# Early stages of a four-layer cross-attention kernel: first buffers loaded one stage ahead, setup in order of need, output projection of self attention rewritten two batches deep

## What is computed

```
x = rms_norm(hidden_states, ln_in_w)
mixed = where(vm, x @ v_qkv, x @ l_qkv)          # vm: token and its follower both of type 1
q, k, v = heads(split(mixed)); q, k = apply_rotary(q, k)
ctx = sdpa(q, k, v, causal=True)                  # 16 heads of 16
hidden_states = residual + where(vm, ctx @ v_dense, ctx @ l_dense)
ci = rms_norm(hidden_states, ln_post_cross_w)
cq = heads(ci @ cq_w);  ck, cv = heads(split(encoder_outputs @ ckv_w))
cctx = sdpa(cq, ck, cv, causal=False)             # 16 heads of 8, 1601 keys
```

## Time and profile before

| | |
|---|---|
| median of 3 runs | 3840.3 us (3838.75 to 3840.41) |
| profiled execution's own time | 3844.03 us |
| its span | 3842.4 us |
| TensorE busy | 3447.9 us (90% of the span) |
| VectorE, ScalarE, GpSimd busy | 2025.7, 1842.6, 1576.5 us |
| transfers | 179.33 MB, mean 47 GB/s |

### The profile page before, as it was taken

One profiled execution on the slowest core, in us unless ns is written; L12 is line 12 of the kernel. 1 busy time (PEld: TensorE's weight loads), 2 busy tenths in 40 slices (PEclk: granted clock), 3 DMA queues, 4 the chain that ended last, 5 costly groups with the idle time before them and its releaser, 6 DMA issues. The chain is left out here.

```text
span 3842.4 us, 74386 instructions
## 1 busy us (share of the span) xinstructions
PE 3447.9 (90%) x25040; PEld 2329.4 (61%) x25040; DVE 2025.7 (53%) x3336; ACT 1842.6 (48%) x3376; POOL 1576.5 (41%) x1401
## 2 busy tenths in 40 slices
PE   5678667989899979997999999999999997998998
PEld 4534443444444438885666666666666665887886
DVE  3435325777777745543556555555555553113544
ACT  1123223766666753433555555555555554233332
POOL 1201021111122211110777777777777777003554
PEclk9878877999999989998999999999999998999998
DMA  3477120000000012223000000000000001202200
GB/s 96 117 109 106 62 94 4 17 16 16 18 17 17 8 64 105 92 101 119 10 13 32 31 13 32 13 31 13 32 13 30 15 12 58 94 33 105 86 13 12
DMA packets 77020, 179.33 MB, mean 47 GB/s; under 512 B 16864, under 2 KB 46048, under 8 KB 71136
## 3 DMA queue, kind: packets, MB, share of 16 engines
q1 hardware_dynamic: 72928, 161.83, 14.4%
q0 software_dynamic: 3712, 12.59, 1.2%
HBM read 115.09 MB, written 59.26 MB: 45 GB/s over the span
## 5 line engine op out<-in xcount | busy, mean ns | idle before, releaser
L1640 POOL TENSOR_TENSOR cross_acc<-cross_acc,cross_probs 128x512 f32<-128x512 f32 (+1 forms) x704 | 921.4, 1309 | 158.7 <-ACT cross_probs L1703 116.9
L1703 ACT ACTIVATE cross_probs<-cross_s,cross_bias 128x512 f32<-128x512 f32 (+1 forms) x832 | 530.2, 685 | 487.4 <-PE cross_s L1917 481.5
L1798 DVE TENSOR_REDUCE cross_partmax<-cross_r 128x1 f32<-128x400 f32 (+1 forms) x1024 | 540.9, 570 | 336.4 <-PE cross_r L1887 318.4
L1270 DVE TENSOR_REDUCE cross_partmax<-cross_m 128x2 f32<-128x800 f32 (+1 forms) x512 | 498.0, 992 | 201.6 <-PE cross_m L1379 200.6
L1190 ACT ACTIVATE cross_probs<-cross_s 128x512 f32<-128x512 f32 (+1 forms) x832 | 452.1, 596 | 148.4 <-PE cross_s L1399 147.8
L1930 PE MATMUL cross_av<-cross_probs,cross_v 128*64 128x256 f32 (+1 forms) x3328 | 458.3, 393 | 0.0
L1930 PEld LDWEIGHTS cross_av<-cross_probs,cross_v 128*64 128x64 f32 (+1 forms) x3328 | 199.4, 136 | 172.8 <-ACT cross_probs L1703 74.6
L1410 PE MATMUL cross_av<-cross_probs,cross_v 128*32 128x256 f32 (+1 forms) x3328 | 269.4, 396 | 11.5 <-ACT cross_probs L1190 8.9
L1379 PE MATMUL cross_m<-cross_ks,cross_qd 64*128 64x400 f32 (+1 forms) x1024 | 210.6, 416 | 51.3 <-DVE cross_partmax L1270 46.2
L1911 PE MATMUL cross_s<-cross_q_hi,cross_k_hi 64*128 64x256 f32 (+1 forms) x1664 | 253.5, 299 | 0.0
L1116 POOL TENSOR_TENSOR cross_diag<-c_ident,cross_negmax 128x256 fp32r<-128x256 f32 x128 | 75.9, 615 | 420.7 <-DVE cross_negmax L1278 420.7
(11 more groups left out here) (284 smaller groups left out, 6581.6 us busy)
## 6 DMA issues: line engine op xcount, KB each, us to landing
d_masked_ctx<-tail_ctx_split SPq DMA_DIRECT2D x8, 1602.0 KB, 5.2
d_self_qk<-selfproj_qk_split POOLq DMA_DIRECT2D x32, 256.0 KB
d_cross<-tail_pr SPq DMA_DIRECT2D x8, 1024.0 KB, 5.1
cross_qp<-d_cross SPq DMA_DIRECT2D x64, 128.0 KB
d_cross<-cross_out SPq DMA_DIRECT2D x64, 128.0 KB, 1.8
tail_at<-d_cross SPq DMA_DIRECT2D x8, 1024.0 KB, 5.5
self_qs<-d_self_qk SPq DMA_DIRECT2D x56, 128.0 KB, 8.4
self_ks<-d_self_qk SPq DMA_DIRECT2D x56, 128.0 KB, 9.0
```

The source lines that it names most:

```text
L1270: nc.vector.tensor_reduce(partmax[:, :, jt // 2, jt % 2, i:i + 1], m_pair(M_SET[q], w), AX.X, ALU.max).then_inc(maxed, 1)
L1640: nc.gpsimd.tensor_tensor(acc[0:w, g % 2], left, probs[0:w, slot % NPB], ALU.add).then_inc(added, 1)
L1703: nc.scalar.activation(probs[0:w, (g * KT + t) % NPB], src_, ACT.Exp, scale=XHD ** -0.5, bias=bias[0:w, p, t:t + 1]).then_inc(probs_ready, 1)
L1798: nc.vector.tensor_reduce(partmax[:, m, i:i + 1], r_ps[MAX_BANK[q]][:, 0:KCH[i][1]], AX.X, ALU.max).then_inc(maxed, 1)
```

## The change

It has five parts.

1. `Phase` takes a side: alternate stages allocate from the left or the right end of the on-chip memory, so a stage's first buffers (`SelfprojEarly`, `SelfEarly`, `SelfoutEarly`, `Cross0Early`) can exist while the one before still runs.
2. Setup: the loads for the rotary tables and the mask come first, with a semaphore of their own; x of batches 0 and 1 and the projection's weights are loaded here too; 13 small vectors are loaded through GpSimd's queue; GpSimd makes three casts.
3. The projection stage: after its x loads, SP loads heads and values of batches 0 and 1 and the heads of batch 2. GpSimd waits for the stores of the batch before instead of its own, VectorE's `out_free` wait stands after the turning. Nothing at the stage's end waits for its stores: the stage that loads them does.
4. Self attention: `ahead` loads nothing; near its end weights, x(0) and attention(0) of the next stage are loaded.
5. `residual_norm` becomes `first_layer_output`: x1 is squared and normalised in place of a copy, TensorE's order is attend(j+1), variance(j), project(j-1). Its SP queue loads context, weights and first queries of cross attention, and GpSimd runs `Cross0Early.fill`. Cross attention's first keys come from `k_chunk`.

```diff
     def sb(self, name, shape, dt=F32):
+        return self.stack.enter_context(self.nc.sbuf_tensor(f"{self.name}_{name}", shape, dt, side=self.side))
...
 def load_constants(nc, src, c, ahead):
-                for name in names:
-                    sp.dma_start(c[name][:], c["loads"][name]).then_inc(loaded, 16)
-                sp.dma_start(tok[:], src["tok_mask"].partition_broadcast(P)).then_inc(loaded, 16)
...
+                sp.dma_start(pos_i[:], src["pos"][0].partition_broadcast(P)).then_inc(first_loaded, 16)
+                sp.dma_start(iota[:], src["c_iota"]).then_inc(first_loaded, 16)
+                sp.dma_start(tables[:], src["c_rope"]).then_inc(first_loaded, 16)
+                sp.dma_start(tok[:], src["tok_mask"].partition_broadcast(P)).then_inc(first_loaded, 16)
+                for name in names[:8]:
+                    sp.dma_start(c[name][:], c["loads"][name]).then_inc(loaded, 16)
+                ahead.load(sp, 0)
+                sp.dma_start(sel[:], src["c_sel"]).then_inc(loaded, 16)
+                ahead.weights(sp)
+                sp.dma_start(causal[:], src["c_causal"]).then_inc(loaded, 16)
+                ahead.load(sp, 1)
+            @block.gpsimd
+            def _(pool):
+                for name in names[8:]:
+                    pool.dma_start(c[name][:], c["loads"][name]).then_inc(vectors_loaded, 16)
+                pool.wait_ge(loaded, 16 * n_loads)
+                nc.gpsimd.tensor_copy(c["causal"][:], causal[:]).then_inc(cast, 1)
...
 def self_projections(nc, src, c, ph, early, ahead_, qk_d, v_d):
+                ahead_.wait_stored(sp, 0)
+                for g in range(NG):
+                    ahead_.heads(sp, 0, slice(2 * g, 2 * g + 2), ahead_.first_loaded[g])
+                    if g == 0:
+                        ahead_.values(sp, 0)
+                ahead_.wait_stored(sp, 1)
+                ahead_.heads(sp, 1, slice(0, NP), ahead_.q_loaded[1])
+                ahead_.values(sp, 1)
+                ahead_.wait_stored(sp, 2)
+                ahead_.heads(sp, 2, slice(0, NP), ahead_.q_loaded[2])
...
-                        pool.wait_ge(q_stored[p], i * 64 + 64)
-                        pool.wait_ge(v_stored[p], i * 16 + 16)
+                    if 0 < b < B - 1:
+                        pool.wait_ge(q_stored[1 - p], 64 * ((b + 1) // 2))
+                        pool.wait_ge(v_stored[1 - p], 16 * ((b + 1) // 2))
                         pool.sem_inc(out_free, 1)
...
-                    dve.wait_ge(out_free, b + 1)
+                    dve.wait_ge(lo_ready, b - 1 + PRIME)
...
                     dve.wait_ge(turned, b * 4 + 4 + PRIME)
+                    dve.wait_ge(out_free, b + 1)
                     nc.vector.tensor_copy(qk_split[:, p, 0], qk[:, p]).then_inc(hi_ready, 1)
...
 def self_attention(nc, c, ph, early, ahead_, out_d):
+                        if b == B - 3:
+                            ahead_.weights(sp)
+                            ahead_.load_x(sp, 0)
...
 def first_layer_output(nc, c, ph, early, ahead, x1_d, q_d):
+                early.load_attn(sp, 1)
+                early.load_x(sp, 1)
+                ahead.load_context(sp)
+                for j in range(-1, B + 1):
+                    l, x, q = batch(j + 2), batch(j), batch(j - 1)
+                    if l is not None and l > 1:
+                        sp.wait_ge(ae_ready, l - 1)
+                        early.load_attn(sp, l)
+                        sp.wait_ge(x1_ready, l - 1)
+                        early.load_x(sp, l)
+                    if x is not None:
+                        sp.wait_ge(x1_ready, x + 1)
+                        sp.dma_start(x1_d[x], x1[:, x % 2]).then_inc(x_stored[x % 2], 16)
+                    if q is not None:
+                        sp.wait_ge(pr_copied, 2 * q + 2)
+                        sp.dma_start(q_d[q], pr[:, q % 2].bitcast(F32)).then_inc(q_stored[q % 2], 16)
+                    if q == 1:
+                        sp.wait_ge(q_stored[0], 16)
+                        ahead.load_queries(sp)
...
+            @block.gpsimd
+            def _(pool):
+                ahead.fill(nc, pool, c)
...
+                split_experts(0)
+                split_experts(1)
+                residual(0)
+                for j in range(B + 1):
+                    if batch(j + 1) is not None:
+                        residual(j + 1)
+                    if batch(j + 2) is not None:
+                        split_experts(j + 2)
+                    if batch(j) is not None:
+                        normalise(j)
+                    if batch(j - 1) is not None:
+                        for m in range(2):
+                            query_low(j - 1, m)
...
+                attend(0)
+                for j in range(B + 1):
+                    if batch(j + 1) is not None:
+                        attend(j + 1)
+                    if batch(j) is not None:
+                        variance(j)
+                    if batch(j - 1) is not None:
+                        project(j - 1)
...
+    def fill(self, nc, pool, c):
+        nc.gpsimd.memset(self.qd[:].bitcast(F32), 0.0).then_inc(self.qd_set, 1)
+        nc.gpsimd.memset(self.v[:], 0.0).then_inc(self.v_set, 1)
+        nc.gpsimd.memset(self.v[:, :, :, :, CHD:CHD + 1], 1.0).then_inc(self.v_set, 1)
+        nc.gpsimd.tensor_tensor(self.wk_hi[:], self.wk[:], c["ones"][:, 0:1].to_broadcast([P, NG * P]), ALU.mult
+        nc.gpsimd.tensor_tensor(self.wk_lo[:], self.wk[:], self.wk_hi[:], ALU.subtract).then_inc(self.wl_ready, 1)
+        for i in range(NC):
+            self.context_chunk(nc, pool, c, 0, 0, i)
...
-                                k_chunk_first(v_, i, h)
+                                k_chunk(v_, i, h)
```

More of the change, by code:

```diff
@@ L965, in statistics, with project @@
                     for k in range(DC):
-                        last = nc.tensor.matmul(var_ps[0][:, 0:S], c["mean"][:], sq[:, k], start=(k == 0), stop=(k == DC - 1))
+                        last = nc.tensor.matmul(var_ps[:, 0:S], c["mean"][:], sq[:, k], start=(k == 0), stop=(k == DC - 1))
                     last.then_inc(var_ready, 1)
-                def project(u):
-                    b, p, _, _ = u
-                    if not kp:
-                        return
-                    pe.wait_ge(xn_ready, b + 1 + PRIME)
-                    for m in range(kpp):
-                        counted(pe, pr_copied, b * kpp + m - 3 if kpp >= 4 else (b - 1) * kpp + m + 1)
-                        for h in range(pair):
-                            t = pair * m + h
+                def project(b):
+                    pe.wait_ge(xn_ready, b + 1)
+                    for m in range(2):
+                        wait(pe, pr_copied, 2 * b + m - 3)
+                        for h in range(2):
+                            t = 2 * m + h
@@ L1148, in step @@
                         context_parts(b + 1, 1 - p)
-                units(pool, NG, ahead, step)
+                units(pool, NG, diagonals, step)
             @block.scalar
@@ L2063, in first_layer_tail @@
     KP = NP // 2
-    with Phase(nc, "tail0") as ph:
+    with Phase(nc, "tail0", "right") as ph:
         wa = ph.sb("wa", [P, D])
```

589 lines of the change are left out of this document (232 added, 357 removed).

## The result

The changed kernel takes 3731.06 us (median of 4 runs, 3729.26 to 3736.44) against 3840.36 us (4 runs, 3838.75 to 3842.44): ratio 0.9717, 95% interval 0.9701 to 0.9734. Predicted were 3712, range 3694 to 3742, chance of faster 0.97. The gain is 109 us where 128 was forecast. In span it is 3842.4 - 3727.5 = 114.9 against 128.5, and the stages say where the rest is.

A forecast was written before the change was run, and what follows sets the result against it. It took late loads and stores at four stage seams, a transfer-set self-attention stretch and TensorE gaps in the output projection as bounds. In span 3842.4 - 20.5 - 47 - 45 - 16 = 3713.9, hence 3712 us, range 3694 to 3742.

The forecast's parts named there:

- Setup and the projection's start: Critical loads first end setup at 18.9 us instead of 33.69, and the first square comes sooner: -20.5 us.
- The projection itself: q/k/v projection: TensorE's pace is its own work, so it stays unchanged.
- rival 5: Projection: VectorE's `hi` waits for earlier stores and stretches batches, making the kernel slower, 3853 us at 70 us landings; chance 0.02.
- The seam: Projection to self attention: barrier follows GpSimd's last issue by 0.9 us, stage starts at 167.1 instead of 176.7; part of -47.
- rival 4: Seam to self attention: the barrier waits for transfers under way, so stores and loads are paid again, 3742 us; chance 0.04.
- The first units: Self attention's start: with early heads, batch 3's heads are issued 36 us into the stage; with the seam -47 us.
- The five periods: Self attention, batch 3's heads onward: five batches in 134 us, set by transfers the change leaves in place.
- The output projection: Early loads and back-to-back matmuls, 8.3 us a batch, bring the stage from 126.5 to 81.2 us: -45.
- The foreseen stall: Output projection, iteration 2: eight `qd` loads issued ahead of at(5) make it land about 3.5 us late.
- Rival 2: Output projection paced by SP's queue, 11.5 us a batch instead of 8.3, total 3734 us; chance 0.14.
- Cross attention's start: Context and weights ready early, four key pairs at 3.5 us, values' matmul 14.1 us into the stage instead of 30.1: -16.
- Rival 1: DMA engines saturate in the projection, batches 1 and 2 arrive only in self attention, total 3724 us; chance 0.12.

The follow-up runs named there:

- E10: E7 plus, in setup, the loads of `sel` and `causal` ahead of x and the weights; 3687.53 us, 0.9609 of the kernel before.
- E1: Changed kernel with the heads of batches 1 and 2 and values of batch 1 loaded at self attention's start again; span 3729.4 us.
- E2: Changed kernel with the five stores of the projection's last batch issued by ScalarE instead of GpSimd; span 3724.3 us.
- E4: Changed kernel with the edits of E2 and E3 together; span 3725.2 us.
- E6: E5 with self attention's output stores issued by GpSimd instead of SP; self attention took 205.9 us.
- E7: E5 with four output buffers instead of two in self attention; 3688.93 us.
- E9: Changed kernel with four output buffers instead of two in self attention, nothing else; 3711.16 us.
- E12: Kernel before the change with four output buffers in self attention and nothing else; 3813.03 us.
- E5: E4 with cross attention's query loads issued behind the store of batch 5's queries instead of batch 1's; 3722.17 us.
- E8: Changed kernel with its output projection one batch deep (var(j), pr(j), at(j+1)), early loads kept; 3772.05 us.
- E3: Changed kernel with SP's projection queue laid out anew: heads directly behind late x loads, 50 issues instead of 98; span 3728.4 us.
- E11: Changed kernel run again as it is, beside the others on one chip; 3734.66 us.

## Why the prediction was right and where it failed

By its own steps, in the span (3713.9 predicted, 3727.5 measured, 13.6 more):

- **Setup and the projection's start, -20.5; measured -18.1**, inside its ends (first square at 22.62, predicted about 20). The landing was put at 16 and was 17.9, since `causal` stood behind the weights; E10 won it back by order alone. The three GpSimd casts took 1.6, predicted 1.9. The barrier took 1.8, predicted 0.9.
- **The projection itself** was taken as unchanged. From first square to the end of the last store's issue it was 124.1 us, 125.5 before: right. No batch was stretched by the wait of `hi`, so rival 5 did not come up.
- **The seam: this is the step that failed.** It said "At the end nothing waits for the last stores: the barrier follows GpSimd's last issue (166.2) by 0.9". It followed by 19.1 us, 18.2 more. What the runs put in its place is the table above: with stores of GpSimd's own under way the barrier opens 2.6 to 2.7 us after the last has landed. It is rival 4's mechanism, to which I gave 0.04, with another price: 18.2 us, not 29.6, since SP's loads under way are not waited for. They cost by slowing those stores, from 7.0 us to landing (E1) to 17.1. A second number behind this step was wrong too: SP's 98 loads were to take 45 us of issue and took 64.7 (91.14 to 155.84), since issues of up to 2.4 us stood among those of 0.42. So SP was not through 11 us before GpSimd but 9 us after it, and E2, where GpSimd held nothing, still opened only at 156.16. E4 needed both edits to reach the predicted seam. The evidence I held against rival 4, seams that open within 1 to 4 us, came from stages where GpSimd has no DMA under way at the end; it could not speak to this one. The one seam that could was on record: in the kernel before, v's store landed at 171.8 and the barrier opened 4.9 us later, not 0.9.
- **The first units, the other part of the -47.** The heads of batch 3 are issued at 199.47, 33.6 us into the stage, predicted 36. Right, 2.4 us better. But from the projection's last matmul to these heads the kernel before took 90.2 us (159.87 to 250.06) and the one after 58.2 (141.23 to 199.47): -32 for seam and first units together instead of -47, outside its own ends.
- **The five periods**: the number was right (133.1 us from 199.47 to the last values' load at 332.59, predicted 134), the reason wrong: it was carried over from the trace before, and came out because the change leaves the order of this queue alone. "That stretch is set by transfers" fell in E6, E7, E9 and E12. What sets it is a store's latency, part SP's queue and part the transfer, against two buffers. A share of 1.03 in a window of 30 us says that the engines are full there, not that the period is.
- **The output projection, -45; measured -48.3.** Steady periods were 7.9 to 8.1 us, predicted 8.3. The foreseen stall came, 3.4 us and 0.9 before it, and E5 showed its cause. E8 showed that depth, not early loading, carries the term. Rival 2 (11.5 us a batch) did not come up.
- **Cross attention's start, -16; measured -16.5** over all that follows. The values' matmuls begin at 473.65, 16.6 us into the stage, predicted 14.1, 30.1 before: 13.5 of the 16.5. The other 3.0 lie behind them, where kernels with the same code differ by more than that (next section), so the close match is in part luck.
- **Rival 1** (batches 1 and 2 late by saturation): the engines did fill (share 1.02 from 141 to 156 us, 1.05 from 156 to 172), yet units 0 to 4 came 5.6 us apart with no wait. The Trainium skill, "DMA: Bandwidth & Descriptors", section "Issuing engines are not separate DMA queues", was the rule weighed there. The stores of GpSimd stretched from 7.0 to 17.1 us beside SP's loads agree with it.

The errors sum up: +2.4 setup, -1.4 projection, +18.2 seam, -2.4 first units, +0.5 rest of self attention, -3.0 output projection, -0.5 cross: 13.8, and 13.6 was measured. The measured 3731.06 lies inside the range, but in the part above 3724 that was there for rivals (1), (2) and (4): of these only the mechanism of (4) came, in part and at a smaller price.

## The clock's scatter, and what stays open

E2 to E4 won 8.9 to 15.8 us at the seam and ended 2.3 to 3.2 us (E2, E4) below the kernel after, or 0.9 above it (E3). Part of this is no effect of theirs, since kernels with the same code differ as much. The same self-attention code took 213.0 us in the kernel after, 215.3 in E11 and 217.7 in E8; the same output projection 78.2 and 80.6. The granted clock differs in these stretches. The windows from 12 to 16 us into self attention, the kernel after:

```profile
177.86:181.86 4.00, 3.49 (x34) 1.81 (x32) 1.32 (x3) 1.25 (x2) 0.00 (x0) 0.88 0.00 0
```

and E2:

```profile
168.16:172.16 4.00, 4.00 (x24) 2.02 (x22) 1.02 (x2) 1.25 (x2) 0.00 (x0) 0.50 0.96 223
```

The clock reads 0.88 in the one, 0.50 in the other (1.2 GHz throughout), which gets to 1.00 only 20 us into the stage; its unit 0 comes 2.0 us later. But the clock's rise is only part of it: unit 0 comes 19.8 us into the stage in the kernel after, 21.8 in E11 and 22.7 in E8, which leaves 0.4 and 1.9 us of the differences for the units behind. And the stages behind the output projection, which none of these edits touches, took 3268.8 to 3275.9 us in the kernel after, E11, E1 to E4, E8 and E9; in E4 they took 5.4 us more than in the kernel after. So a single run can't price a seam of 9 us in the whole. That the seam's gain reaches the end when the stalls are gone too is seen in E7 against E9: 22.3 us of span, of which 14.1 at the seam and 4.5 in the output projection. How much of E2's and E4's missing gain is scatter and how much a real give-back was not settled: each was timed once. Open too is what GpSimd does at a barrier after its transfers have landed.

## What to carry to other kernels

Before a barrier, ask which engine issued the transfers of the stage: in this program GpSimd's held it, at one seam until they had landed and at another 10 us longer, and what SP or ScalarE issued did not. So try the stage's last stores on another queue than GpSimd's, and look at the barrier again after moving stores onto GpSimd. Where one write in four waits for a store and the transfer engines look full, add a buffer before believing in bandwidth: here it was worth 20 us on the changed kernel (23 against E11, timed beside it) and 28 on the kernel before. Evidence against a rival counts only from places where the rival's condition holds.

## What the runs showed of the hardware that was not expected

- The barrier opened 2.6 to 2.7 us after the landing of GpSimd's last own store in six runs of five kernels, 4.9 after it in the kernel before, and 10 us after it in E6, where all engines and transfers had been idle since 345.5 us. It opened 1.1 us after the last issue where SP or ScalarE issued last, in E2 with the DMA engines full (share 1.03 and 1.07 around it).
- SP's issues, mostly 0.42 us each, took up to 2.4 us in the projection stage of the kernel after, so 98 of them took 64.7 us.
- A VectorE cast of 128x128 took 0.65 us beside a GpSimd cast and 0.23 alone; a GpSimd cast of 128x512 took 1.99 us beside a VectorE operation on two inputs (12.43 to 14.71 in E10; the cast ran until 15.19) and 0.61 beside a cast. The Trainium skill, "SBUF — State Buffer", section "SBUF: two separate sides", says that the two engines share a port pair as an exclusive lock; the rows agree in direction, and no run here isolates the lock.
- The matmuls behind a gap of some 2 to 3 us ran longer: 16 records 5.4 us in E8 and 6.7 in E4, 3.6 undisturbed. In the kernel after a gap of 3.36 us cost nothing of that kind.
